# One output tile at a time in the attention, GpSimd's row transfers spread over the tiles, and the last sums on TensorE

## The reference, cut to what matters

```python
x = x + 0.5 * ffn(layernorm(x))      # 4 x 1024 rows of 128
x = x + attn(layernorm(x))
x = x + 0.5 * ffn(layernorm(x))      # the same weights

def ffn(t):                          # 8 experts, the best 2 of each row
    logits = t @ Wr.T + br
    w = softmax(top 2 of logits)
    o = sum over the 2: w * (relu(t @ W1[e].T + b1[e]) @ W2[e].T + b2[e])
    return layer_norm(t + o) * gamma + beta

def attn(x):                         # differential attention, per batch of 1024 rows
    q1, q2 = split(x @ w_q12); k1, k2 = split(x @ w_k12); v = x @ w_v
    diff = softmax(q1 @ k1.T * s) - lam * softmax(q2 @ k2.T * s)
    out = diff @ v
    return out / sqrt(mean(out * out) + eps) * 0.2
```

## Time and profile before

| | |
|---|---|
| time, median of 3 runs | 793.73 us (790.54 to 795.02) |
| time of the profiled execution | 794.53 us |
| its span | 792.8 us |
| mean granted clock of TensorE | 0.876 of full speed |
| first pass, tiles 0 to 77 | about 97 to 290 us of the span |
| attention, first maximum to last transpose | 298.8 to 545.3 us |
| second pass, first to last tile | 567.0 to 758.1 us |
| tail | 758.1 to 792.8 us |

### The profile page before, as it was taken

One profiled execution on the slowest core, in us unless ns is written; L12 is line 12 of the kernel. 1 busy time (PEld: TensorE's weight loads), 2 busy tenths in 40 slices (PEclk: granted clock), 3 DMA queues, 4 the chain that ended last, 5 costly groups with the idle time before them and its releaser, 6 DMA issues.

```text
span 792.8 us, 16016 instructions
## 1 busy us (share of the span) xinstructions
PE 597.0 (75%) x3864; PEld 518.2 (65%) x3864; DVE 459.3 (58%) x1446; ACT 437.2 (55%) x1107; POOL 374.5 (47%) x467
## 2 busy tenths in 40 slices
PE   2634277799779987799799699787669559999910
PEld 2623266799779875566566577563669449999810
DVE  4535523264336649868959976963245325557746
ACT  4334144366546564685785785753366236696733
POOL 6437044500342523764763454767553654555633
PEclk9955597799999999999899989997899869999965
DMA  8302223322233310100010000012221122422041
GB/s 284 118 28 74 50 71 82 88 69 75 68 82 82 78 38 1 30 24 6 22 27 1 0 18 21 27 58 57 60 57 48 58 67 76 152 72 67 27 163 55
DMA packets 54249, 49.16 MB, mean 62 GB/s; under 512 B 9926, under 2 KB 45938, under 8 KB 53904
## 3 DMA queue, kind: packets, MB, share of 16 engines
q1 hardware_dynamic: 45312, 31.25, 13.9%
q0 software_dynamic: 8640, 16.87, 6.9%
q10 hardware_dynamic: 208, 0.02, 0.0%
HBM read 25.99 MB, written 23.02 MB: 62 GB/s over the span
## 4 chain that ended last, share of the span: by engine, by line
PE 49%; DVE 19%; issue 11%; another core or an unknown queue 8%; ACT 7%; POOL 3%; DMA 2%; ACTq 1%; DVEq 0%; POOLq 0%; SPq 0%
PE banks L891 17%; PE banks L901 16%; DVE nb L1483 4%; PE banks L884 2%; PE banks L823 2%; DVE scratch L1492 2%; PE banks L825 2%; PE banks L824 2%; PE banks L970 2%; ACT scratch L611 1%; DVE st_r L1124 1%; PE banks L869 1%; ACT rowbuf L568 1%; PE banks L858 1%
## 5 line engine op out<-in xcount | busy, mean ns | idle before, releaser
L901 PE MATMUL banks<-blocks,scratch 128*128 x1248 | 176.3, 287 | 30.8 <-issue 25.7
L901 PEld LDWEIGHTS banks<-blocks,scratch 128*128 128x128 f32 x1248 | 161.7, 202 | 33.9 <-issue 33.7
L1261 DVE TENSOR_SCALAR scratch<-banks,blocks 128x128 f32<-128x128 f32 x312 | 95.1, 345 | 148.9 <-PE banks L891 75.5
L891 PE MATMUL banks<-scratch 128*128 128x128 f32 x1248 | 177.4, 288 | 3.4 <-ACT scratch L611 2.1
L891 PEld LDWEIGHTS banks<-scratch 128*128 128x128 f32 x1248 | 162.0, 203 | 7.9 <-issue 7.4
L605 ACT ACTIVATE scratch<-banks 128x128 f32<-128x128 f32 x156 | 43.3, 278 | 155.6 <-PE banks L884 79.5
L448 POOL DMA_INDIRECT rows<-rowbuf,slot x96 | 95.6, 996 | 56.3 <-issue 49.7
L470 POOL DMA_INDIRECT results<-scratch x78 | 78.1, 1001 | 77.1 <-DVE scratch L1269 43.3
L459 POOL DMA_INDIRECT zb<-yrows,slot x64 | 64.8, 1013 | 99.2 <-DVE scratch L1269 80.8
L618 ACT ACTIVATE scratch<-banks,blocks 128x128 f32<-128x128 f32 x312 | 96.8, 366 | 25.9 <-PE banks L891 14.4
L674 ACT ACTIVATE scratch<-banks,nb 128x1024 f32<-128x1024 f32 x64 | 71.2, 1113 | 66.3 <-DVE nb L1483 60.8
(11 more groups left out here) (187 smaller groups left out, 866.7 us busy)
## 6 DMA issues: line engine op xcount, KB each, us to landing
scratch<-rows SPq DMA_DIRECT2D x156, 64.5 KB
yrows<-scratch SPq DMA_DIRECT2D x78, 64.0 KB
rows<-padrows SPq DMA_DIRECT2D x34, 64.5 KB
x<-in_L_attn_x_dram SPq DMA_DIRECT2D x4, 512.0 KB, 5.5
scratch<-in_L_ffn_W_dram SPq DMA_DIRECT2D x1, 2048.0 KB, 19.2
rows<-rowbuf,slot POOLq DMA_INDIRECT x96
results<-scratch POOLq DMA_INDIRECT x78
zb<-yrows,slot POOLq DMA_INDIRECT x64
```

The lines of the kernel that those rows point to most:

```text
L891: ins = pe.matmul(hT_at(T, c), staged(T, c), xT_of(T), start=True, stop=True)
L901: ins = pe.matmul(y_at(T), hT_of(T, c), blocks[:, W2_AT + c * D:][:, bass.ds(at, D)], start=(c == 0), stop=(c == FC - 1))
L1261: ins = dve.tensor_scalar(hT_of(T, c), hT_at(T, c), blocks[:, B1_AT + c:][:, bass.ds(at, 1)], 0.0, ALU.add, ALU.max)
```

## The change

It has seven parts.

1. **Attention outputs per tile.** v = xn w_v is computed once per batch (`multiply_Wv`, 8 matmuls of 128 columns; ACT copies it, `copy_v`; for it ACT also copies the transposed rows unrounded, `copy_xnT_whole`). Then `values(b, i)` gives the outputs of one query tile at once, 8 matmuls of 128 columns with the tile's `dT` as weights. `o_copy`, `squares` and DVE's reciprocals of the sums are gone; `take_o` copies and squares each tile's output on ACT. `value_scale` has four operations instead of three and works from the unnormalised output.
2. **Order within the attention.** Scores, transposes and values of one tile each now alternate on PE. DVE's added values and their statistics move two tiles later; in the last batch `choose` moves behind the last `difference`, and ACT's `copy_rows` behind the last `dT_copy`.
3. **Preparation of attention inside the first pass.** Transposing and splitting batch 0's rows moves into tiles 73 to 77 (`turn_first_xn`, `copy_first_xnT`, `first_xnT_rest`). The merge starts at tile 52 instead of 49, with a denser table, and the normalisation is at tiles 72 to 75 instead of 74 to 77.
4. **Scatters of the first pass**: one behind each y of tiles 0 to 31.
5. **Scatters of batch 2 at the second pass's entry**: three, then `rstd`, three more, and one behind each of the first ten sends.
6. SP no longer waits for `ss_ready` before it loads the second pass's first tile; batch 3's statistics, transposes and choice are one to two tiles earlier.
7. **Tail**: the sums with `tgt` and three of the four sums with x are matmuls with the identity into PSUM (512 columns, float32); ACT copies the finished x (`give`).

```diff
-        STATS_AT, TURN_AT = 2, 9
+        STATS_AT, TURN_AT = 0, 8
...
             sp.wait_ge(dT_ps, TB * BATCHES)
-            sp.wait_ge(ss_ready, GROUPS * (BATCHES - 1) + 1)
...
             for s in range(SLOTS):
                 wait_apart(pool, (y_sb, s + 1))
-                if s < PAIRS:
-                    i = 2 * s % PAIRS
-                    scatter(0, GB + s // TB, range(i, i + 2))
+                if s < 2 * PAIRS:
+                    i = s % PAIRS
+                    scatter(0, GB + s // PAIRS, range(i, i + 1))
...
-            scatter(1, BATCHES - 2, range(14))
             value_scale(BATCHES - 1, 1)
-            scatter(1, BATCHES - 2, range(14, PAIRS))
+            scatter(1, BATCHES - 2, range(3))
+            rstd(n)
+            scatter(1, BATCHES - 2, range(3, 6))
             for s in range(SLOTS):
                 send(s)
-                if s == STATS_AT:
-                    rstd(n)
+                if s < PAIRS - 6:
+                    scatter(1, BATCHES - 2, range(s + 6, s + 7))
...
+            def take_o(b, i):
+
+                c = slice(i * D, (i + 1) * D)
+                act.wait_ge(o_ps, TB * b + i + 1)
+                if b:
+                    act.wait_ge(values_added, GROUPS * (b - 1) + i // QG + 1)
+                act.activation(osb[:, c], bank(6, 0, D), ACT.Copy)
+                act.activation(osq[:, c], bank(6, 0, D), ACT.Square, scale=(OUT_GAIN / D) ** 0.5, accum_out=ss[:, i:i + 1]).then_inc(ss_ready, 1)
...
+            def multiply_Wv(b):
+
+                pe.wait_ge(xnT_sb, b + 2)
+                if b:
+                    pe.wait_ge(dT_sb, TB * b)
+                for k in range(TB):
+                    ins = pe.matmul(bank(4 + k // 4, k % 4 * P, (k % 4 + 1) * P), xnT[:, k * P:(k + 1) * P], wv[:, :], start=True, stop=True)
+                ins.then_inc(v_ps, 1)
+
+            def values(b, i):
+
+                t = TB * b + i
+                pe.wait_ge(dT_sb, t + 1)
+                if t:
+                    pe.wait_ge(ss_ready, t)
+                for k in range(TB):
+                    ins = pe.matmul(bank(6, 0, D), dT[t % 2][:, k * P:(k + 1) * P], vb[:, k * D:(k + 1) * D], start=(k == 0), stop=(k == TB - 1))
                 ins.then_inc(o_ps, 1)
...
+            def half_sum(b, h):
+
+                pe.matmul(sum_bank(b, h), ident[:, :], half_of(tgt, b, h), start=True, stop=False)
+                pe.wait_ge(weighted, GB + 2 * (b - GB) + h + 1)
+                pe.matmul(sum_bank(b, h), ident[:, :], half_of(sums[b], None, h), start=False, stop=True).then_inc(summed, 1)
+
+            def half_out(b, h):
+
+                pe.matmul(out_bank(b, h), ident[:, :], half_of(x, b, h), start=True, stop=False)
+                pe.wait_ge(gained, 2 * (b - GB) + h + 1)
+                pe.matmul(out_bank(b, h), ident[:, :], half_of(sums[b], None, h), start=False, stop=True).then_inc(whole, 1)
```

More of the change, by code:

```diff
@@ L513, in _ @@
                 for i in range(TB):
+                    if i == TB - 1:
+                        value_scale(b, 0)
+                    if last and i == 2:
+                        value_scale(b - 1, 1)
                     ratio(b, i)
@@ L517, in _ @@
                         n += 1
-                    if last and i == 2 + after:
-                        value_scale(b - 1, 1)
-                    if last and i == 3 + after:
+                    if last and i == 3:
                         rstd(n)
@@ L720, in attention @@
                     copy_xm(b + 1)
-                    squares(b, 0)
-                else:
-                    o_copy(b, 0)
-                    gap(a)
-                    squares(b, 0)
-                    copy_rows(1, b - 1)
-                if last and after:
-                    copy_tgtT(a, 1)
-                dT_copy(b, TB - 2)
+                    dT_copy(b, TB - 2)
+                    if last:
+                        copy_tgtT(a, 1)
+                else:
+                    dT_copy(b, TB - 2)
+                    take_o(b, TB - 3)
+                if not after:
+                    dT_copy(b, TB - 1)
+                    copy_rows(1, b - 1)
+                    take_o(b, TB - 2)
+                    gap(a)
+                    take_o(b, TB - 1)
                 return n + 2 * after + last
@@ L809, in _, with give @@
                         rescale(f, range(4 * scale, 4 * scale + 4))
+            def give(b, h):
+                i = 2 * (b - GB) + h
+                act.wait_ge(whole, i + 1)
+                act.activation(x[:, b * TB * D + h * TB * D // 2:][:, 0:TB * D // 2], out_bank(b, h), ACT.Copy).then_inc(x_done, 1)
             weigh(2, halves_of(0))
@@ L1501, in attention @@
                         xnT_rest(b + 1)
-                    if not after and i == TB - 1:
-                        read_logits(a)
-                        at_once(choose(a))
                     if b > 1 and i == 0:
                         read_logits(a - 1)
-                    if last and i == 0:
-                        add_values(b - 1, 0)
                     if after and i == 0:
@@ L1529, in attention @@
                         n += 1
+                    if not after and i == TB - 1:
+                        add_values(b, 0)
                 if after:
```

313 lines of the change are left out of this document (172 added, 141 removed).

## The result

The changed kernel took 772.2 us (median of 4 runs, 770.5 to 774.3), against 793.7 for the kernel before: ratio 0.974, 95% interval 0.970 to 0.978. It is faster by 21.5 us. The forecast was faster by 41, 753.5 us; the time lies in the range, nearer to the rival of 777. The profiled execution has a span of 768.8 us, 24.0 less than before, and that difference is what the table splits up. All stretches run from one y of a tile to another, or to the first maximum of a batch of the attention.

What follows compares the result with a forecast made beforehand. No engine was taken to bound the whole span; the passes lose time where POOL issues transfers back to back. Terms of -18, -2.5, -7.5, -14, +2.5 and -1.5 sum to -41: from 794.5 to 753.5 us, range 737 to 778.

Steps and rivals of the forecast that it cites:

- the rival of 777: Whole kernel: time goes per transfer however spaced, so the first pass's spacing gains 0; 777 us, chance 0.10.
- First pass, tiles 1 to 32: One scatter per tile leaves no train: 2.05 us a tile, less 2.4 us charged for late rows; -18 us, ends 0 and -24.
- Into the attention: First pass to attention: PE's 3.6 us gap goes as batch 0's transposes move into tiles 73 to 77; -2.5 us, ends -5 and +3.
- Batches 0 to 2: Attention: values per tile fill PE's waits for ACT's exponential, 2.5 us a batch; -7.5 us, ends -18 and +12.
- Batch 3 and entry: Attention's end to second pass: ACT's copy wait, late values and a scatter train go, `choose` adds 1; -14 us, ends -22 and -4.
- (c): Second pass's entry: the train of 16 scatters, holding PE 5.37 us ahead of its first L901, becomes three scatters; -5.4 us.
- Tiles 1 to 16 of the second pass: Thirteen moved scatters return as a train of about 26 transfers; +2.5 us for the `ln_stats` wait, ends -6 and +12.
- Tail: Kernel's end: DVE sheds 4.7 us of sums, PE gets 14 matmuls of 512 columns; -1.5 us, ends -5 and +4.
- Per transfer, not per train: Whole kernel: each transfer costs its time however spaced, so the first pass gains 0; 777 us, chance 0.10.
- Compute does not yield at all: Whole kernel: POOL's transfers do not hold compute; slow tiles have another cause, such as SP's loads; 777 us, chance 0.04.
- Group 1's rows late: First pass: PE waits for most of the six tiles by which SP starts later; 763 us, chance 0.10.
- The new chain of a tile binds: Attention: PE stands at `values` for the previous tile's squares on ACT, in all 32 tiles; 805 us, chance 0.04.

## Why the prediction was right or wrong

**First pass, tiles 1 to 32: right in mechanism, undersized.** Predicted -18, measured -25.8, beyond the end of -24; the working began from 86.0 us where it was 86.5. Nothing in these tiles shows scatters at all: 1.90 us a tile, where I took 2.05 by a mean of two rows, and the 2.4 us that I charged for late rows don't fall in these tiles.

**Tiles 33 to 77: the missing term.** I saw that SP would stand at tile 39 with its writes queued behind it, and priced it as a short wait of PE for tile 39. PE never waited for that. What waited was POOL, for the writes, and what followed was the gathers as a train: +10.5 us. I had charged the delay and not asked what it would bunch up.

**Into the attention:** predicted -2.5, measured -4.6, near the end of -5.

**Batches 0 to 2: wrong.** Predicted -7.5, measured +0.5. PE's wait for the exponential fell by 7.5 us as said, and no wait for the squares of note came up (1.4 us). But the new order puts `dT_copy` ahead of the next batch's transposes in the shared banks, 7.1 us against 1.6, and DVE's waits for ACT's copies of these transposes (L1535) rose from 1.1 to 6.4 us. I priced the tiles of a batch and not its last step. This is an account by waits, not by an experiment.

**Batch 3 and entry:** predicted -14, measured -13.9, which is in part luck. Of its parts (c), the train's 5.4 us, isn't a gain of the spread, as the run with the old entry shows: y of tile 0 is as early without it. The other parts must have brought 5 us more than I gave them, and no run takes them apart.

**Tiles 1 to 16 of the second pass: a size off, at the range's end.** Predicted +2.5, measured +12.4; I had +12 as the bound. The working had the train of about 26 transfers, 15 us over the undisturbed pace; the stall of tile 7 alone is 18.4 us. The credit that I gave, that before had lost as much there, was wrong: before, a good part of the stall lay ahead of y of tile 0, where PE stood 5.37 us and ACT 6.71:

```profile
553.08 0.28 ACT L605 ACTIVATE scratch<-banks 128x128 f32<-128x128 f32 x1 [6.71 <-issue]
```

Batch 3, entry and these tiles together (88.5 + 45.7, now 74.6 + 58.1) gained 1.5 us where I had 11.5.

**Tail:** -2.4 for -1.5.

**The total.** Of the 17 us by which the profile's -24.0 misses -41, the attention's batches 0 to 2 have 8 and tiles 1 to 16 of the second pass 10. In the first pass two misses, -7.8 and +10.5, cancelled to 2.7. That the time lies in the range owes something to this.

**The rivals.** "Per transfer, not per train" is refuted by three runs, though its 777 us is nearer the result than my figure. "Compute does not yield at all", which the Trainium skill's page "SBUF — State Buffer", section "Who interferes with whom", would have, is refuted on chips A, with 14.13 us of ACT as the clearest row; on chips B it describes what the profile shows. Whether the ports of which the page speaks have a part in it no run shows. "Group 1's rows late" didn't happen as written, since PE never stood for tile 39 in the first pass; SP's delay did cost about as much, through POOL's gathers. "The new chain of a tile binds" didn't happen. The range held because its upper part was drawn to take in late rows and a part of the attention's loss.

**What stays open.** Why the engines stop. Excluded: a cost per transfer, the kind of transfer (trains of scatters, of gathers, and of sends with scatters all do it), and a wait for instructions on their way. The register reads are not needed for it, as DVE's 11.04 us ahead of the first tile show. What distinguishes chips A from B is open too.

## What to carry to other kernels

Count the transfers that GpSimd will issue without a break at run time, not in the program's order: after any wait on its queue it makes up what it missed, and a train of eight or more can hold the other engines, on chips A, until it ends. Where a queue (here SP's) has both loads and writes in it, ask who stands behind the writes when a load waits; here POOL stood there, and not PE. And measure on more than one chip before you tune against such a stall: what brings 2.6% here brings 1.1% there.

## What the runs showed of the hardware

- The same kernel takes 794 to 796 us on some chips and 696 to 699 on others, with runs 0.6 to 1.3% apart on one chip. In the changed kernel, which I have in profiles of both, all but a few us of the difference lie where GpSimd issues transfers back to back.
- On a chip A, with a break of 1.1 us after each three of 24 transfers, twelve tiles took 30.7 us at full clock instead of 46.0, with no stall over 4.4 us; after each four it brought 1 us in sixteen tiles, and 1.7 us brought 10.
- The stalls need no register read and no late instructions: DVE stood 11.04 us for PE's logits in a train, and SP's arithmetic on one register took 626 ns (median of five) in a train on A, 37 ns on B.
- On a chip B POOL issued 68 transfers without a break, 1.27 us apart, and the engines ran beside them at full clock.
- The stall costs clock as well: granted 0.82 and 0.78 in the second pass's two stretches with trains on a chip A and 0.91 in the first pass's, 1.00 in the same stretches on B.
